# Routed experts of a mixture layer: the up product with stationary weights from two ScalarE-filled buffers, token weights applied at the last eviction

## The chip, the cores and the metric

The kernel runs on one core of a Trainium2 chip. The metric is the device time of one execution in microseconds (us); the kernel before takes 927.88 us, the median of three runs (925.97, 927.88 and 929.93).

## The reference

Two decoder layers on 16 sequences of 128 tokens with 256 features, all in fp32: linear attention, cross attention, and a routed attention-and-FFN block in the first layer, softmax attention, cross attention and a mixture of experts in the second, with a layer norm after each. The change lies in the mixture of experts. Each of the 2048 tokens goes to 4 of 16 routed experts (group-limited top-k of sigmoid scores, normalised, times 2.5); in addition every token goes through two shared experts of the same size. Cut to what matters:

```
combine = (one_hot(topk_idx, E) * tw[..., None]).sum(1)     # token weight per expert
h = einsum('td,edf->etf', x, gate_w)                        # D = 256, F = 256, E = 16
u = einsum('td,edf->etf', x, up_w)
y = einsum('etf,efd->etd', silu(h) * u, down_w)
routed = einsum('etd,te->td', y, combine)
out = routed + shared
```

The token weight is one number per token and expert, so it may stand on silu(h)*u or on y.

## The kernel before, in words

The program is written engine by engine: each engine has its own in-order list of instructions, and semaphores ("steps") tie the lists together. Everything ahead of the mixture's routed part, and the final sums and layer norms behind it, are the same in both kernels.

**The routed part.** Tokens have been scattered by expert into a DRAM table `grid`, so that the work falls into NSLOT = 79 slots of 128 rows, each with one expert. `f_se` holds the expert number of each slot and `f_src` the tile of the table. All experts' weights lie in SBUF in `W[P, expert, 1536]`: for each of the KC = 2 halves k of the 256 input features, 512 columns (256 of gate, 256 of up), and behind them 2 x 256 columns of down. A slot t goes through these steps:

- SyncE (L794 to L799) reads the tile number into a register (`value_load`, L797) and loads the 128 rows into a ring of 8 buffers.
- PE `q_turn_` (L1579) transposes the rows, two transposes of 128x128 (helper line L1059) into PSUM bank t%2; ScalarE `q_turned_` (L1931, L1934) copies them to `f_xT`.
- PE `q_up_` (L1585) reads the expert number with `value_load` (L1586) and multiplies: `f_xT` is the stationary operand (two tiles of 128x128), the expert's weights are the moving operand, 512 columns wide, read from `W` at an address in a register (helper line L1046). The result, tokens on the partitions, gate in columns 0 to 255 and up in columns 256 to 511, lies in bank 2 + t%2.
- ScalarE `q_silu_` (L1926, L1929) takes the silu of the gate half; VectorE `q_mul_` (L2538, L2542) multiplies it by the up half and by the token weight `s_w`, which VectorE `q_w_` (L2531, L2534) picks out of the row that came with the tokens.
- PE `q_back_` (L1597) transposes the product (two more transposes, L1059) into bank 4 + t%2 and ScalarE `q_backed_` (L1937, L1940) copies it to `f_aT`, since the down product contracts over the 256 hidden features.
- PE `q_down_` (L1603), with a `value_load` of its own (L1604), multiplies `f_aT` (stationary) by the down weights, 256 columns wide, into bank 6 + t%2; VectorE `q_y_` (L2546, L2552) copies that to a ring of 4 buffers and GpSimd `q_scatter_` (L999, L1006) adds it to the rows of `ys` in DRAM by an indirect DMA.

**Order.** `rolled(engine, stages, ...)` (L251) writes an engine's list: in iteration i it emits, in the order of the given list, each stage for slot i minus its lag. The middle slots are a hardware loop that is unrolled 8 times. The lists are

```
PE    (q_up_, 1), (q_back_, 2), (q_turn_, 0), (q_down_, 3)
ACT   (q_silu_, 1), (q_backed_, 2), (q_turned_, 0)
DVE   (q_mul_, 1), (q_w_, 0), (q_y_, 3)
```

so in iteration i PE does up(i-1), back(i-2), turn(i), down(i-3), and ScalarE silu(i-1), backed(i-2), turned(i). A `wait(engine, step, t, 1, back=2)` asks for the step of slot t-2, as a double buffer needs. A first semaphore of a stage is waited for by the instruction itself; an engine does nothing that stands behind a waiting instruction in its list. A fp32 product of one 128x128 stationary tile is issued as two passes, each a weight load (PEld) and a matmul; a transpose is one pass.

Of the kernel before, what the change touches and what calls it, by code (L numbers as in the profile page):

```python
# [22 lines left out]
P = 128  # L23
B = 16
D = 256
KC = D // P
# [19 lines left out]
E = 16  # L46
EF = 256
# [4 lines left out]
NSLOT = B * 4 + E - 1  # L52
# [5 lines left out]
SR, YR, UR = 8, 4, 8  # L58
# [143 lines left out]
def wait(eng, step, t, k, back=0):  # L202

    if t.peeled and t.b + step.turns * step.round < back:
        return
    eng.wait_ge(step.sem, step.at(t, k, back))
# [44 lines left out]
def rolled(eng, stages, start, total):  # L251


    deepest = max(lag for _, lag in stages)

    def iteration(i):
        for stage, lag in stages:
            if 0 <= i - lag < total:
                stage(Slot(i - lag, i - lag, 0))

    for i in range(start):
        iteration(i)
    with eng.Fori(start // UR, total // UR) as j:
        for u in range(UR):
            for stage, lag in stages:
                stage(Slot(UR * j + (u - lag), u - lag, j))
    for i in range(total // UR * UR, total + deepest):
        iteration(i)
# [14 lines left out]
def build(nc, a):  # L283
    out = a["out"]
    with ExitStack() as ctx:
# [6 lines left out]
        def step(name, n, turns=B, tiles=0):  # L292
            return Step(sem(name), n, 0, turns, tiles)

        bank = [ctx.enter_context(nc.psum_tensor(f"bank{i}", [P, 512], F32)) for i in range(8)]
# [4 lines left out]
        rows = sb("rows", [P, N_ROWS])  # L300
# [45 lines left out]
        A = Carve(0)  # L346
# [47 lines left out]
        A = Carve(0)  # L394
# [28 lines left out]
        A = Carve(kx_at)  # L423
        c_oTs = [A(NQ, S) for _ in range(TILES)]
        A = Carve(folded_at)
# [3 lines left out]
        A = Carve(weights_end)  # L429
        c_S = [A(H, S) for _ in range(TILES)]  # L430
        A = Carve(weights_end)
        c_gT = A(FC, TILES * S)
        A = Carve(weights_end)
# [4 lines left out]
        A = Carve(0)  # L438
# [12 lines left out]
        f_xT = A(B, KC, P)  # L451
# [55 lines left out]
        assert A.at <= scores_at + 2 * H * P  # L507
        A = Carve(scores_at)
        f_h = [A(EF) for _ in range(2)]
        f_a = [A(KC * EF)]  # L510
        f_aT = [A(KC, P) for _ in range(2)]
        A = Carve(0)
        t_bn, t_mv = A(B, 6), A(B, 2)
        t_std, t_rstd, t_off, t_shift = A(B), A(B), A(B), A(B)
# [149 lines left out]
        q_xp = step("q_xp", 1, NSLOT)  # L664
        q_xc = step("q_xc", 1, NSLOT)
        q_up = step("q_up", 1, NSLOT)
        q_silu = step("q_silu", 1, NSLOT)
        q_w = step("q_w", 1, NSLOT)
        q_mul = step("q_mul", 1, NSLOT)
        q_ap = step("q_ap", 1, NSLOT)  # L670
        q_ac = step("q_ac", 1, NSLOT)
        q_dp = step("q_dp", 1, NSLOT)
        q_yc = step("q_yc", 1, NSLOT)

# [356 lines left out]
        def _(pe):  # L1031
# [10 lines left out]
            def product(o, lhs, rhs):  # L1042

                n = len(lhs)
                for k in range(n):
                    m = pe.matmul(o, lhs[k], rhs[k], start=k == 0, stop=k == n - 1)  # L1046
                return m
# [9 lines left out]
            def transposes(o, src, n, width):  # L1057
                for k in range(n):
                    m = pe.transpose(o[:, k * width:(k + 1) * width], src(k), ident[0:width, 0:width])  # L1059
                return m  # L1060
# [522 lines left out]
                    .then_inc(q_xp.sem, 1)  # L1583

            def q_up_(t):  # L1585
                e = pe.value_load(f_se[0:1, bass.ds(t.b, 1)], min_val=0, max_val=E - 1)  # L1586
                wait(pe, q_xc, t, 1)
                wait(pe, q_mul, t, 1, back=2)
                if t.peeled and t.b == 0:
                    pe.wait_ge(l_w[0], 16 * 9)  # L1590
                    pe.wait_ge(l_w[1], 16 * 7)
                    wait(pe, h_yc, turn(DONE - 2), 1)
                product(bank[2 + t.p][:], [f_xT[:, t.p, k, :] for k in range(KC)],
                        [W[:, bass.ds(e, 1), 2 * k * EF:2 * (k + 1) * EF].rearrange("p a n -> p (a n)")
                         for k in range(KC)]).then_inc(q_up.sem, 1)

            def q_back_(t):  # L1597
                wait(pe, q_mul, t, 1)
                wait(pe, q_ac, t, 1, back=2)
                transposes(bank[4 + t.p][:, 0:D], lambda k: f_a[0][:, t.p * EF + k * P:t.p * EF + (k + 1) * P], KC, P)\  # L1600
                    .then_inc(q_ap.sem, 1)

            def q_down_(t):  # L1603
                e = pe.value_load(f_se[0:1, bass.ds(t.b, 1)], min_val=0, max_val=E - 1)  # L1604
                wait(pe, q_ac, t, 1)
                wait(pe, q_yc, t, 1, back=2)
                if t.peeled and t.b == 0:
                    wait(pe, h_yc, turn(DONE - 1), 1)
                product(bank[6 + t.p][:, 0:D], [f_aT[t.p][:, k, :] for k in range(KC)],
                        [W[:, bass.ds(e, 1), (4 + k) * EF:(5 + k) * EF].rearrange("p a n -> p (a n)")  # L1610
                         for k in range(KC)]).then_inc(q_dp.sem, 1)

            pe.wait_ge(f_routed, 5)
            rolled(pe, [(q_up_, 1), (q_back_, 2), (q_turn_, 0), (q_down_, 3)], UR, NSLOT)

            def t_down_(b):
                mine = slice((b - DONE) * P, (b - DONE + 1) * P)
# [16 lines left out]
        def _(act):  # L1634
# [299 lines left out]
                act.copy(f_xT[:, t.p], bank[t.p][:, 0:D].rearrange("p (k t) -> p k t", k=KC))\  # L1934
                   .then_inc(q_xc.sem, 1)

            def q_backed_(t):  # L1937
                wait(act, q_ap, t, 1)
                wait(act, q_dp, t, 1, back=2)
                act.copy(f_aT[t.p], bank[4 + t.p][:, 0:D].rearrange("p (k t) -> p k t", k=KC))\  # L1940
                   .then_inc(q_ac.sem, 1)

            wait(act, h_dp, turn(DONE - 1), 1)
            rolled(act, [(q_silu_, 1), (q_backed_, 2), (q_turned_, 0)], UR, NSLOT)

            for u in range(DONE, UNITS):
                h_silu_(turn(u))
# [7 lines left out]
        def _(dve):  # L1955
# [574 lines left out]

            def q_w_(t):  # L2531
                dve.wait_ge(l_sx[t.ring(SR)], 16 * (t.lap(SR) + 1))
                wait(dve, q_mul, t, 1, back=2)
                dve.scalar_tensor_tensor(out=s_pick[t.p], in0=s_x[t.ring(SR)][:, D:D + E], scalar=1.0,  # L2534
                                         in1=f_mine[:, bass.ds(t.b, 1), :].rearrange("p a e -> p (a e)"),
                                         op0=ALU.mult, op1=ALU.mult, accum_out=s_w[t.p]).then_inc(q_w.sem, 1)

            def q_mul_(t):  # L2538
                wait(dve, q_silu, t, 1)
                wait(dve, q_ap, t, 1, back=2)  # L2540
                wait(dve, q_w, t, 1)
                dve.scalar_tensor_tensor(out=f_a[0][:, t.p * EF:(t.p + 1) * EF], in0=f_h[t.p],  # L2542
                                         scalar=s_w[t.p], in1=bank[2 + t.p][:, EF:2 * EF],
                                         op0=ALU.mult, op1=ALU.mult).then_inc(q_mul.sem, 1)

            def q_y_(t):  # L2546
                wait(dve, q_dp, t, 1)
                if not t.peeled or t.b >= YR:
                    dve.wait_ge(l_sy[t.ring(YR)], 16 * t.lap(YR))
                elif t.b >= YR - HR + 2:  # L2550
                    dve.wait_ge(l_hs[t.b - YR + HR], 16 * (DONE // HR))
                dve.tensor_copy(s_y[t.ring(YR)], bank[6 + t.p][:, 0:D]).then_inc(q_yc.sem, 1)  # L2552

            rolled(dve, [(q_mul_, 1), (q_w_, 0), (q_y_, 3)], UR, NSLOT)

            def t_sum_(b):
                dve.wait_ge(l_sx[b // 2], 16 * ((NSLOT + SR - 1 - b // 2) // SR + 1))
# [110 lines left out]
```

## Time and profile before

| what | value |
|---|---|
| median of three runs | 927.88 us (925.97 to 929.93) |
| profiled execution: span, first to last instruction | 927.1 us |
| median minus that span | 0.8 us |
| PE busy over the span | 851.1 us, 92% |
| VectorE, ScalarE, GpSimd busy | 561.4, 438.7, 458.6 us |
| mean granted TensorE clock | 0.980 of 2.4 GHz |
| routed slots: first silu, last silu | 641.09 us, 889.77 us |

The profile has no whole-program time of its own for the profiled execution beside its span; the span is 0.8 us (0.1%) under the median of the runs. In its page, PE is the matmul part of TensorE and PEld its weight loads, which overlap; the end of a matmul is modelled. The timeline merges neighbouring instructions of one line, with the number of them behind an x; in brackets stands how long the engine had been idle and who released it. Views of a line give the number of instructions, the shortest, median and longest duration in ns and the first and the last start.

### The profile page before, as it was taken

Reading aid. Unit: us, or ns where it says so; the run is one execution under the profiler, and the core shown is the slowest. Engines: PE = TensorE matmul, PEld = TensorE weight load, DVE = VectorE, ACT = ScalarE, POOL = GpSimd, SP = SyncE. Lnnn points to the kernel's source line nnn. Section 1 sums busy time; section 2 is a strip of 40 time slices with the busy share of each in tenths; the row PEclk is TensorE's granted clock in tenths of the full one; section 3 lists DMA queues with packets and bytes.
Section 4 is the critical chain, followed back from the end, with each engine's and each line's share of the span. In section 5 each row is a group of like instructions: output and inputs, shape, how many; then the busy total and the mean of one; then the engine's idle time right before and its main releaser. Section 6 shows DMA issues by size and latency. Waiting matters only on the chain.

```text
span 927.1 us, 20122 instructions
## 1 busy us (share of the span) xinstructions
PE 851.1 (92%) x5868; PEld 609.7 (66%) x5869; DVE 561.4 (61%) x1640; ACT 438.7 (47%) x1159; POOL 458.6 (49%) x609
## 2 busy tenths in 40 slices
PE   5989689997988999998999988998899999999995
PEld 2666479875877888887777765555455555555553
DVE  3799638849126989888887898583233333333325
ACT  2556345445526777777777864211232323223224
POOL 3999512103135454633455444777744545454545
PEclk9999989998999999999999999999899999999998
DMA  8610111000039999981511100756445555555547
GB/s 300 197 67 6 34 30 36 24 18 12 24 89 308 290 314 326 277 238 41 201 36 37 36 30 32 273 206 213 103 83 92 84 88 88 85 92 83 94 60 253
DMA packets 86642, 113.50 MB, mean 122 GB/s; under 512 B 8224, under 2 KB 77600, under 8 KB 86048
## 3 DMA queue, kind: packets, MB, share of 16 engines
q1 hardware_dynamic: 71392, 90.49, 32.1%
q0 software_dynamic: 14448, 19.34, 12.9%
q10 hardware_dynamic: 720, 2.63, 0.8%
q8 instruction: 44, 0.72, 0.3%
q14 instruction: 38, 0.31, 0.1%
HBM read 48.40 MB, written 64.05 MB: 121 GB/s over the span
## 4 chain that ended last, share of the span: by engine, by line
PE 71%; DVE 7%; POOL 7%; issue 6%; ACT 4%; DMA 4%; SPq 0%; POOLq 0%; DVEq 0%; ACTq 0%
PE bank L1046 46%; PE bank L1059 7%; PE bank L1522 6%; PE bank L1495 3%; PE bank L1532 3%; POOL arena L896 2%; POOL arena L877 1%; DMA ys<-arena 1%; DMA const<-in_const 1%; DVE arena L2436 1%; POOL arena L872 1%; PE bank L1390 1%; PE bank L1232 1%; PE bank L1038 1%; DMA arena<-ys 1%
## 5 line engine op out<-in xcount | busy, mean ns | idle before, releaser
L1046 PE MATMUL bank<-arena 128*128 (+6 forms) x1344 | 423.1, 455 | 16.8 <-ACT arena L1683 8.9
L1046 PEld LDWEIGHTS bank<-arena 128*128 128x128 f32 (+1 forms) x1344 | 230.3, 191 | 131.1 <-issue 96.2
L1006 POOL DMA_INDIRECT ys<-arena x79 | 123.2, 1559 | 117.3 <-DVE arena L2552 103.0
L2542 DVE SCALAR_TENSOR_TENSOR arena<-arena,bank 128x256 f32<-128x256 f32 x79 | 38.0, 481 | 143.8 <-ACT arena L1929 143.8
L1929 ACT ACTIVATE arena<-bank 128x256 f32<-128x256 f32 x79 | 30.4, 385 | 176.0 <-PE bank L1046 176.0
L1059 PEld LDWEIGHTS bank<-const,arena 128*128 128x128 f32 x572 | 69.7, 142 | 66.3 <-issue 56.8
L855 POOL TENSOR_TENSOR lr<-mv,const 128x1 f32<-128x1 f32 x48 | 9.2, 192 | 187.9 <-DVE mv L1978 187.8
L2436 DVE TENSOR_REDUCE arena<-bank 128x4 f32<-128x512 f32 x128 | 87.0, 680 | 23.7 <-PE bank L1495 12.1
L1059 PE MATMUL bank<-const,arena 128*128 128x128 f32 x572 | 94.2, 277 | 6.6 <-DMA arena<-grid 2.6
L1889 ACT ACTIVATE arena<-arena 128x512 f32<-128x512 f32 x116 | 74.1, 638 | 38.0 <-DVE arena L2442 37.1
L1522 PE MATMUL bank<-const,arena 128*128 128x128 f32 x512 | 79.7, 278 | 4.3 <-ACT arena L1896 3.4
L2442 DVE TENSOR_TENSOR arena<-bank,arena 128x512 f32<-128x512 f32 x116 | 80.3, 692 | 4.0
L1896 ACT COPY arena<-bank 128x512 f32<-128x512 f32 x128 | 75.9, 593 | 12.7 <-PE bank L1522 11.8
L950 POOL DMA_INDIRECT grid<-X,arena x64 | 63.3, 989 | 20.2 <-issue 18.5
L1046 PE MATMUL bank<-arena,inT 128*128 128x256 f32 (+1 forms) x192 | 59.5, 434 | 10.1 <-DMA arena<-in_a_w 5.9
L1522 PEld LDWEIGHTS bank<-const,arena 128*128 128x128 f32 x512 | 56.7, 141 | 18.1 <-issue 13.5
L1046 PE MATMUL bank<-xT,arena 128*128 128x128 f32 x512 | 66.2, 278 | 2.2 <-ACT xT L1655 2.2
L1046 PEld LDWEIGHTS bank<-xT,arena 128*128 128x128 f32 x512 | 61.8, 194 | 3.0 <-ACT xT L1655 3.0
L2552 DVE COPY arena<-bank 128x256 f32<-128x256 f32 x79 | 33.6, 425 | 30.9 <-PE bank L1046 29.0
L1046 PEld LDWEIGHTS bank<-arena,inT 128*128 128x128 f32 x192 | 34.0, 197 | 19.5 <-issue 11.9
L974 POOL TENSOR_TENSOR arena<-arena,const 128x256 f32<-128x256 f32 x64 | 38.1, 616 | 5.0 <-ACT arena L1871 5.0
L1532 PE MATMUL bank<-arena 128*32 128x128 f32 x1024 | 34.6, 275 | 3.4 <-ACT arena L1896 3.2
(288 smaller groups left out, 1339.1 us busy)
## 6 DMA issues: line engine op xcount, KB each, us to landing
grid<-arena SPq DMA_DIRECT2D x1, 37264.0 KB, 132.0
arena<-in_f_w SPq DMA_DIRECT2D x18, 768.0 KB, 7.2
arena<-grid SPq DMA_DIRECT2D x79, 137.0 KB, 2.7
arena<-ys SPq DMA_DIRECT2D x8, 512.0 KB, 8.0
inT<-in_ctxT SPq DMA_DIRECT2D x30, 128.0 KB, 2.0
X<-in_x SPq DMA_DIRECT2D x1, 2048.0 KB, 15.6
arena<-in_c_w SPq DMA_DIRECT2D x2, 1024.0 KB, 5.0
ys<-arena SPq DMA_DIRECT2D x1, 2048.0 KB, 10.3
```

Source lines behind the costliest of these rows:

```text
L950: pool.indirect_dma_start(grid, bass.IndirectOffsetOnAxis(ap=f_to[:, b, k:k + 1], axis=0), X[:, b, :], None).then_inc(l_sc[b % 3], 16)
L974: pool.tensor_tensor(d_kx[t.p][:, k], kT[:, k:k + 1, :].to_broadcast([P, 2, P]), c("pairs").unsqueeze(2).to_broadcast([P, 2, P]), ALU.mult ...
L1006: pool.indirect_dma_start(ys, bass.IndirectOffsetOnAxis(ap=number, axis=0), s_y[t.ring(YR)], None, compute_op=ALU.add).then_inc(l_sy[t.rin ...
L1046: m = pe.matmul(o, lhs[k], rhs[k], start=k == 0, stop=k == n - 1)
L1059: m = pe.transpose(o[:, k * width:(k + 1) * width], src(k), ident[0:width, 0:width])
L1522: m = pe.transpose(bank[7][:, i * P:(i + 1) * P], d_S[t.p][:, QH * r + i, :], ident)
L1532: m = pe.matmul(bank[0][32 * i:32 * i + 32, g * P:(g + 1) * P], d_v[t.p][:, QH * g + i, :], d_pT[t.p][:, QH * g + i, :], start=True, stop= ...
L1889: act.activation(v, v, ACT.Exp).then_inc(d_exp.sem, 1)
L1896: act.copy(d_pT[t.p][:, QH * r:QH * (r + 1), :], bank[7][:].rearrange("p (a b) -> p a b", a=QH)).then_inc(d_pTc.sem, 1)
L2436: dve.tensor_reduce(mx, s_, AX.X, ALU.max).then_inc(dm.sem, 1)
L2442: dve.tensor_tensor(d_S[t.p][:, QH * r:QH * (r + 1), :], s_, mx.unsqueeze(2).to_broadcast([P, QH, P]), ALU.subtract).then_inc(dm.sem, 1)
L2542: dve.scalar_tensor_tensor(out=f_a[0][:, t.p * EF:(t.p + 1) * EF], in0=f_h[t.p], scalar=s_w[t.p], in1=bank[2 + t.p][:, EF:2 * EF], op0=ALU ...
```

## The change

The up product changes operands: 128x128 pieces of the expert's gate and up weights become the stationary operand and the transposed tokens the moving one, so its result has the hidden features on the partitions and feeds the down product without the transposes back. The stationary pieces are read from two fixed buffers `f_up[t%2]` (in the space of `rows`, no longer used by then), into which ScalarE copies the 1024 gate and up columns of the expert, at an address that it reads itself with `value_load`. The token weight moves from the product of silu and up to the eviction of the down product. `q_back_` and `q_backed_` are gone, the down product's lag is 2 in place of 3.

```diff
-        f_a = [A(KC * EF)]
         f_aT = [A(KC, P) for _ in range(2)]
+        f_up = [rows[:, i * 2 * KC * EF:(i + 1) * 2 * KC * EF] for i in range(2)]
...
             def q_up_(t):
-                e = pe.value_load(f_se[0:1, bass.ds(t.b, 1)], min_val=0, max_val=E - 1)
                 wait(pe, q_xc, t, 1)
+                wait(pe, q_wc, t, 1)
                 wait(pe, q_mul, t, 1, back=2)
...
-                product(bank[2 + t.p][:], [f_xT[:, t.p, k, :] for k in range(KC)],
-                        [W[:, bass.ds(e, 1), 2 * k * EF:2 * (k + 1) * EF].rearrange("p a n -> p (a n)")
-                         for k in range(KC)]).then_inc(q_up.sem, 1)
-
-            def q_back_(t):
-                wait(pe, q_mul, t, 1)
-                wait(pe, q_ac, t, 1, back=2)
-                transposes(bank[4 + t.p][:, 0:D], lambda k: f_a[0][:, t.p * EF + k * P:t.p * EF + (k + 1) * P], KC, P)\
-                    .then_inc(q_ap.sem, 1)
+                for half in range(2):
+                    for part in range(KC):
+                        at = half * EF + part * P
+                        m = product(bank[2 + t.p][:, at:at + P],
+                                    [f_up[t.p][:, 2 * k * EF + at:2 * k * EF + at + P] for k in range(KC)],
+                                    [f_xT[:, t.p, k, :] for k in range(KC)])
+                m.then_inc(q_up.sem, 1)

             def q_down_(t):
                 e = pe.value_load(f_se[0:1, bass.ds(t.b, 1)], min_val=0, max_val=E - 1)
-                wait(pe, q_ac, t, 1)
+                wait(pe, q_mul, t, 1)
                 wait(pe, q_yc, t, 1, back=2)
...
-            rolled(pe, [(q_up_, 1), (q_back_, 2), (q_turn_, 0), (q_down_, 3)], UR, NSLOT)
+            rolled(pe, [(q_up_, 1), (q_turn_, 0), (q_down_, 2)], UR, NSLOT)
...
-            def q_backed_(t):
-                wait(act, q_ap, t, 1)
-                wait(act, q_dp, t, 1, back=2)
-                act.copy(f_aT[t.p], bank[4 + t.p][:, 0:D].rearrange("p (k t) -> p k t", k=KC))\
-                   .then_inc(q_ac.sem, 1)
+            def q_weights_(t):
+                if t.peeled and t.b == 0:
+                    act.wait_ge(f_routed, 5)
+                    act.wait_ge(l_w[0], 16 * 9)
+                    act.wait_ge(l_w[1], 16 * 7)
+                e = act.value_load(f_se[0:1, bass.ds(t.b, 1)], min_val=0, max_val=E - 1)
+                wait(act, q_up, t, 1, back=2)
+                act.copy(f_up[t.p], W[:, bass.ds(e, 1), 0:2 * KC * EF].rearrange("p a n -> p (a n)")).then_inc(q_wc.sem, 1)

-            rolled(act, [(q_silu_, 1), (q_backed_, 2), (q_turned_, 0)], UR, NSLOT)
+            rolled(act, [(q_silu_, 1), (q_turned_, 0), (q_weights_, 0)], UR, NSLOT)
...
             def q_w_(t):
                 dve.wait_ge(l_sx[t.ring(SR)], 16 * (t.lap(SR) + 1))
-                wait(dve, q_mul, t, 1, back=2)
+                wait(dve, q_yc, t, 1, back=2)
...
             def q_mul_(t):
                 wait(dve, q_silu, t, 1)
-                wait(dve, q_ap, t, 1, back=2)
-                wait(dve, q_w, t, 1)
-                dve.scalar_tensor_tensor(out=f_a[0][:, t.p * EF:(t.p + 1) * EF], in0=f_h[t.p],
-                                         scalar=s_w[t.p], in1=bank[2 + t.p][:, EF:2 * EF],
-                                         op0=ALU.mult, op1=ALU.mult).then_inc(q_mul.sem, 1)
+                wait(dve, q_dp, t, 1, back=2)
+                dve.tensor_tensor(f_aT[t.p], f_h[t.p].rearrange("p (k t) -> p k t", k=KC),
+                                  bank[2 + t.p][:, EF:2 * EF].rearrange("p (k t) -> p k t", k=KC), ALU.mult)\
+                   .then_inc(q_mul.sem, 1)
...
-                dve.tensor_copy(s_y[t.ring(YR)], bank[6 + t.p][:, 0:D]).then_inc(q_yc.sem, 1)
-
-            rolled(dve, [(q_mul_, 1), (q_w_, 0), (q_y_, 3)], UR, NSLOT)
+                wait(dve, q_w, t, 1)
+                dve.tensor_scalar(s_y[t.ring(YR)], bank[6 + t.p][:, 0:D], s_w[t.p], None, ALU.mult).then_inc(q_yc.sem, 1)
+
+            rolled(dve, [(q_mul_, 1), (q_y_, 2), (q_w_, 0)], UR, NSLOT)
```

## Rows read from the trace of the kernel before

**Rows 1.** The page: busy time by engine, and its shares of 40 slices.

```profile
PE 851.1 (92%) x5868; PEld 609.7 (66%) x5869; DVE 561.4 (61%) x1640; ACT 438.7 (47%) x1159; POOL 458.6 (49%) x609
...
PE   5989689997988999998999988998899999999995
```

**Rows 2.** Windows: span, busy (count) of PE, PEld, DVE, ACT, POOL, clock, DMA.

```profile
700.00:880.00 180.00, 180.00 (x696) 105.81 (x695) 57.93 (x232) 53.62 (x174) 89.89 (x59) 1.00 0.54 87
```

**Rows 3.** Timeline of one slot: start, duration, engine, line, count.

```profile
700.30 0.37 ACT L1940 COPY arena<-bank 128x256 f32<-128x256 f32 x1
...
700.55 0.39 ACT L1934 COPY arena<-bank 128x256 f32<-128x256 f32 x1
...
702.91 0.60 PE L1059 MATMUL bank<-const,arena 128*128 128x128 f32 x4
...
703.11 0.39 ACT L1929 ACTIVATE arena<-bank 128x256 f32<-128x256 f32 x1 [2.17 <-PE bank L1046]
...
703.35 1.03 PE L1046 MATMUL bank<-arena 128*128 x4
703.39 0.37 ACT L1940 COPY arena<-bank 128x256 f32<-128x256 f32 x1
703.53 0.48 DVE L2542 SCALAR_TENSOR_TENSOR arena<-arena,bank 128x256 f32<-128x256 f32 x1 [1.78 <-ACT arena L1929]
```

**Rows 4.** Timeline in an attention stage: eight 128-column fp32 passes in a row.

```profile
455.10 1.06 PE L1046 MATMUL bank<-xT,arena 128*128 128x128 f32 x8
```

**Rows 5.** Groups by line and form: busy us, mean ns, idle before.

```profile
L1059 PE MATMUL bank<-const,arena 128*128 128x128 f32 x572 | 94.2, 277 | 6.6 <-DMA arena<-grid 2.6 <-DVE arena L2046 2.0 <-ACT arena L1903 1.1
L1046 PE MATMUL bank<-arena 128*128 128x256 f32 x336 | 84.8, 387 | 10.4 <-ACT arena L1683 8.9 <-DVE arena L2397 1.5
...
L1046 PE MATMUL bank<-arena 128*128 128x512 f32 x160 | 72.2, 594 | 0.0
L1046 PE MATMUL bank<-xT,arena 128*128 128x128 f32 x512 | 66.2, 278 | 2.2 <-ACT xT L1655 2.2
```

**Rows 6.** Groups of ScalarE: the rows nearest to a copy of 1024 columns.

```profile
L1896 ACT COPY arena<-bank 128x512 f32<-128x512 f32 x128 | 75.9, 593 | 12.7 <-PE bank L1522 11.8
L1889 ACT ACTIVATE arena<-arena 128x512 f32<-128x512 f32 x116 | 74.1, 638 | 38.0 <-DVE arena L2442 37.1
...
L1655 ACT COPY xT<-bank 128x256 f32<-128x256 f32 x48 | 18.2, 379 | 10.6 <-PE bank L1038 5.5 <-PE bank L1059 5.0
```

**Rows 7.** SyncE's value load (L797) and what uses its register (L798).

```profile
L797 SPq TENSOR_LOAD <-arena x79: 262/267/816, 633.1 to 877.8; - x79
L797 SPq FUSED_REGOPS  x79: 152/152/173, 633.6 to 878.1; - x79
L797 SPq SEQ_ASSERT  x79: 18/18/33, 633.8 to 878.3; - x79
...
L798 SPq MOVE arena<-grid x79: 29/29/37, 634.0 to 878.5; - x79
```

**Rows 8.** PE's value loads between 700 and 880 us.

```profile
L1586 PEldq TENSOR_LOAD <-arena x58: 296/301/314, 699.9 to 877.1; - x58
...
L1604 PEldq TENSOR_LOAD <-arena x58: 298/578/711, 701.5 to 878.9; - x58
```

**Rows 9.** Timeline: the first slots, from the first copy to ScalarE's first silu.

```profile
638.54 0.37 ACT L1934 COPY arena<-bank 128x256 f32<-128x256 f32 x1 [8.32 <-PE bank L1059]
...
639.07 1.98 PE L1046 MATMUL bank<-arena 128*128 x4 [0.62 <-ACT arena L1934]
...
641.09 0.39 ACT L1929 ACTIVATE arena<-bank 128x256 f32<-128x256 f32 x1 [2.17 <-PE bank L1046]
```

**Rows 10.** Timeline: the last silu and the last eviction of a down product.

```profile
889.77 0.39 ACT L1929 ACTIVATE arena<-bank 128x256 f32<-128x256 f32 x1 [2.17 <-PE bank L1046]
...
893.79 0.42 DVE L2552 COPY arena<-bank 128x256 f32<-128x256 f32 x1 [0.58 <-PE bank L1046]
```

**Rows 11.** Timeline: the one interruption of the rhythm.

```profile
662.64 0.39 ACT L1929 ACTIVATE arena<-bank 128x256 f32<-128x256 f32 x1 [2.34 <-PE bank L1046]
...
665.35 0.69 PE L1059 MATMUL bank<-const,arena 128*128 128x128 f32 x2 [2.61 <-DMA arena<-grid]
...
671.87 0.39 ACT L1929 ACTIVATE arena<-bank 128x256 f32<-128x256 f32 x1 [5.42 <-PE bank L1046]
```

**Rows 12.** Windows: stretches in which PE has idle time (columns as in rows 2).

```profile
90.00:98.00 8.00, 4.92 (x31) 3.65 (x29) 7.79 (x23) 5.14 (x17) 5.40 (x7) 1.00 0.13 36
...
102.00:112.00 10.00, 7.75 (x38) 5.94 (x37) 6.79 (x21) 3.94 (x10) 4.87 (x8) 1.00 0.00 0
...
286.00:290.00 4.00, 2.54 (x20) 2.00 (x19) 3.90 (x9) 2.16 (x5) 0.45 (x2) 1.00 0.80 270
...
666.00:672.00 6.00, 5.69 (x11) 3.13 (x11) 0.42 (x1) 0.51 (x2) 3.51 (x3) 0.50 0.69 120
```

More of the change, by code:

```diff
@@ L666, in build @@
         q_up = step("q_up", 1, NSLOT)
+        q_wc = step("q_wc", 1, NSLOT)
         q_silu = step("q_silu", 1, NSLOT)
@@ L669, in build @@
         q_mul = step("q_mul", 1, NSLOT)
-        q_ap = step("q_ap", 1, NSLOT)
-        q_ac = step("q_ac", 1, NSLOT)
         q_dp = step("q_dp", 1, NSLOT)
@@ L1585, in q_up_ @@
             def q_up_(t):
-                e = pe.value_load(f_se[0:1, bass.ds(t.b, 1)], min_val=0, max_val=E - 1)
                 wait(pe, q_xc, t, 1)
+                wait(pe, q_wc, t, 1)
                 wait(pe, q_mul, t, 1, back=2)
                 if t.peeled and t.b == 0:
-                    pe.wait_ge(l_w[0], 16 * 9)
-                    pe.wait_ge(l_w[1], 16 * 7)
                     wait(pe, h_yc, turn(DONE - 2), 1)
-                product(bank[2 + t.p][:], [f_xT[:, t.p, k, :] for k in range(KC)],
-                        [W[:, bass.ds(e, 1), 2 * k * EF:2 * (k + 1) * EF].rearrange("p a n -> p (a n)")
-                         for k in range(KC)]).then_inc(q_up.sem, 1)
-            def q_back_(t):
-                wait(pe, q_mul, t, 1)
-                wait(pe, q_ac, t, 1, back=2)
-                transposes(bank[4 + t.p][:, 0:D], lambda k: f_a[0][:, t.p * EF + k * P:t.p * EF + (k + 1) * P], KC, P)\
-                    .then_inc(q_ap.sem, 1)
+                for half in range(2):
[5 more added lines that the diff above has]
+                m.then_inc(q_up.sem, 1)
             def q_down_(t):
                 e = pe.value_load(f_se[0:1, bass.ds(t.b, 1)], min_val=0, max_val=E - 1)
-                wait(pe, q_ac, t, 1)
+                wait(pe, q_mul, t, 1)
                 wait(pe, q_yc, t, 1, back=2)
```

## The prediction

> **What bounds the kernel now.** I read the page first: PE is busy for 92% of the span, and in the last third of the slices, where the routed slots lie, for 90% or more [rows 1]. Then the windows of the routed part: from 700 to 880 us PE is busy for all of 180 us, at the full clock (1.00, the 2.4 GHz level), while ScalarE works 53.6 us, a third [rows 2]. Then the timeline of one slot. PE's dynamic matmuls of slot after slot begin 3.09 us apart, silu after silu too, and ScalarE waits 2.17 us for PE before each silu [rows 3]. So a slot costs what PE needs for it, and every wait of another engine lies under PE. Over the whole part the first silu starts at 641.09 and the last at 889.77 us [rows 9, 10]: 248.7 us for 78 steps, of which one step of 9.23 us (662.64 to 671.87) is an interruption [rows 11]: PE had to wait 2.61 us for a load of rows, and then worked at half clock.
>
> **What PE gains.** The passes of a slot before: up 4 of 512 columns, transposes 4, down 4 of 256. Four transposes take 0.44 us from the first of them to the matmul behind (702.91 to 703.35), so 0.11 us each; four down passes last 1.03 us with the last one's 0.39 us whole, so 0.215 each and about 0.87 together [rows 3, 5]; a 512-column pass costs 72.2/160 = 0.45 us by its group, or 3.09 - 0.44 - 0.87 = 1.78 us for four [rows 3, 5]. After: up is 8 products of 128 columns, 16 passes. The nearest row is eight such fp32 passes with a new weight tile for each: 1.06 us with the last one's 0.28 us whole, so 0.111 us each [rows 4], and 16 cost 1.78 us. Splitting the product is thus free, the doubled weight loads hide behind the matmuls, and what goes is the two transposes back: 0.22 us a slot, 17 us over 79 slots, if PE stayed the bound. Bounds of the pass: 0.11 (a transpose) to 0.13 us (66.2/512 over the whole group, tails included) [rows 5], so 1.76 to 2.1 us for up.
>
> **What takes its place.** ScalarE's list is in order: silu(i-1), turned(i), weights(i). PE's up(i) needs the weights of slot i, and silu(i-1) needs the whole up(i-1). So the copy of the next slot's weights stands behind a silu that waits for the slot in work. The two buffers don't help: the copy would be free to start two slots ahead, but it is queued behind that wait. The loop is up(i-1), then silu or the transposes, then turned(i), then the value load, then the copy, then up(i), once per slot. I add it up from the start of up(i-1):
>
> - up, 16 passes at 0.111: 1.78 us [rows 4].
> - turn(i), two transposes: the second starts 0.11 later and lasts 0.27; the transposed rows are there at 2.16 us [rows 3, 5]. The silu starts at 1.95 + 0.03 and blocks the engine for 0.28 us only (the next ScalarE instruction starts 0.28 us after it [rows 3]), so turned(i) goes at 2.16 + 0.03 (the hop from an end to the waiting engine: 703.11 + 0.39 to 703.53 [rows 3]) = 2.19.
> - The value load stands behind turned(i) in the list and starts when that is let go. On SyncE it is 0.27 + 0.15 + 0.02 us of instructions, and 0.7 us pass from the start of the load (877.8) to the instruction behind (878.5) [rows 7]. I take 0.75 us, with one register operation ahead for the index. Ends: 0 hidden behind turned's own work (see the rivals), 1.05 if the load takes 0.58 us.
> - The copy of 1024 columns: no row has that width. From 256 to 512 columns a copy grows from 0.379 to 0.593 us, 0.84 us per 1000 columns; to 1024 that gives 1.02 us, from the row with its source in SBUF (0.638) 1.07 us [rows 6]. I take 1.04, and 0.07 us for its start. Ends: 1.0, and 1.19 for twice the row of 512.
> - From the end of a ScalarE copy to PE's matmul: 638.54 + 0.37 to 639.07, 0.15 us [rows 9].
>
> Sum: 2.19 + 0.75 + 0.07 + 1.04 + 0.15 = 4.20 us a slot against 3.09. PE's own work, 1.78 + 0.22 + 0.87 = 2.87 us, fits under it with about 1.3 us idle. PE's one remaining value load (down) runs behind the transposes during ScalarE's part: 2.0 + 1.0 (a load of 0.58 and SyncE's 0.43 for what follows it, [rows 7, 8]) + 0.87 = 3.9 us at worst, still under 4.20.
>
> Of the value load, the rows show 0.267 us on SyncE and 0.30 or 0.58 us at the median at PE's two places [rows 7, 8]; my sum uses the first. The Trainium skill (DMA: Bandwidth & Descriptors, Latency and other measured facts) puts a floor of about 600 ns under a tensor_load. The rows are below that floor; by the page the sum would be 0.33 us a slot higher, an estimate of 1033 us.
>
> **The rest of the change.** VectorE: the multiply loses its scalar and keeps 128x256 (0.48 us), the eviction gains one (0.42 us before [rows 10]); both are one pass over the same elements. VectorE has 57.9 of 180 us of work [rows 2], so it stays covered; if that cover went, 0.1 us would stand in each place. The multiply ends at about 1.98 + 0.42 + 0.48 = 2.9, before down(i-1) of the next round. GpSimd's scatter comes once per 4.2 us in place of 3.09 and has more room; SyncE's loads keep their 8 buffers. ScalarE's work per slot becomes 0.39 + 0.39 + 1.04 us, under half of 4.20: it isn't full, it is in the chain. A longer slot also swallows the interruption: slot 8's rows arrived at 665.35 [rows 11], while PE would ask for them only after 640.6 + 8 x 4.20 = 674 us. That step becomes an ordinary one; the sum below counts it so.
>
> At the front the first up waits for the first weights: 638.57 + 0.75 + 0.07 + 1.04 + 0.15 = 640.6 in place of 639.07 [rows 9], +1.5 us. At the end the last eviction starts 4.0 us after the last silu [rows 10]; with one stage less I take 3.0, -1 us (between -2 and 0).
>
> Total: 78 x 4.20 = 327.6, minus 248.7 is +78.9; +1.5 - 1.0 gives +79.4. The span goes from 927.1 to 1006.5; the median lies 0.8 us above the span, so about 1007 us.
>
> **Rivals.**
>
> *The value load is hidden (15%).* ScalarE's sequencer might run it while silu and turned(i) are in work. For it: their durations overlap (0.25 us from copy to copy, each 0.37 or more [rows 3]). Against: the load stands behind an instruction that waits for the transposes. Then the slot is 1.95 + 0.03 + 0.28 + 0.25 + 1.04 + 0.15 = 3.70 us, +40 us: 968.
>
> *The value load is slow on ScalarE (12%).* PE's second one has a median of 0.578 us [rows 8]; 0.28 us more per slot, 78 x 0.28 = +22: 1029.
>
> *The clock falls (7%).* PE would idle some 1.3 us in each slot. In the trace, the clock went to 0.50 (1.2 GHz) after PE had stood for 2.61 us [rows 11, 12]. Stretches with shorter gaps kept 1.00: PE busy 61% at 90 to 98 us, 78% at 102 to 112, 64% at 286 to 290 [rows 12]; the new slot would be near 70%. At half clock passes double: 2.19 becomes about 4.1 and the slot 6.1 us, 1155 if it never recovers, about 1080 if half the time. The Trainium skill (TensorE: Matmul & The Clock Gate, A second HAM failure mode: psum-queue depth-cycling) tells of a kernel whose clock oscillates because PE idles briefly and often between groups of matmuls, which would speak against this change; the three rows at 1.00 don't bear it out.
>
> *PE stays the bound, and the kernel gets faster (3%).* If the copy of slot i ran while PE works on up(i-1), the slot would be 2.87 us and the 0.06 us that 3.09 holds over its 3.03 of passes (with 1.72 for up): 2.93. 78 x 2.93 = 228.5, and the interruption's 6.1 us stay: 14 us less, 913 us. The mechanism is that of the two buffers; it decides once the copy is ready before PE has done turn(i) and down(i-2). Against it stands ScalarE's order, which leaves no way round the silu. The same with a slot near 3.1 us gives no change (1%).
>
> **How the numbers follow.** Forecast 62%, slot 3.9 to 4.5 us: 984 to 1031, likeliest 1007. A tenth of a us in the slot is 7.8 us. The range of 8 in 10 takes in the hidden load and the slow one: 966 to 1036, leaving out the clock, the faster case and the outer parts of the forecast. 0.5% of 927.9 (4.6 us) is about what a measurement of this kernel can tell from no change. Slower 0.96, within it 0.01, faster 0.03.
>
> **What the profile after would show.** Right: silus 4.2 us apart; before each up pass PE idle about 0.5 to 1.3 us, released by ScalarE's copy of 1024 columns; that copy 1.0 to 1.1 us; a value load on ScalarE's queue between turned and the copy; PE busy near 75% from 700 us on with the clock at 1.00; the wait for rows at 662 us gone. The chain of waits should name ScalarE's copy where it named PE alone. Wrong: silus 3.7 us apart or less (load hidden); PE idle before down rather than before up (PE's own value load binds); a clock below 1.00; or a ScalarE that copies weights before silu's wait is over.

## The result, and the profile after

The changed kernel takes 1017.85 us (median of 4 runs, 1015.5 to 1019.05), the kernel before 928.61 us beside it; the ratio is 1.0957, 95% interval 1.0936 to 1.0978. The forecast was 1007 us in a range of 966 to 1036.

The page of the changed kernel, busy time by engine and PE's shares of 40 slices, against [rows 1]:

```profile
PE 852.2 (84%) x6658; PEld 680.5 (67%) x6659; DVE 567.4 (56%) x1640; ACT 498.6 (49%) x1160; POOL 457.8 (45%) x609
...
PE   6998699979989999999998999777777777777786
```

PE works as long as before, 852 against 851 us, in a span that is 90 us longer: its share in the routed part has gone from 9 and over to 7 tenths. The two transposes that are gone don't show in that sum: a burst of passes that ends in idle time counts its last pass whole, and there is one such burst per slot now. The windows of that part, against [rows 2] (span, then busy time and count of PE, PEld, DVE, ACT, POOL, then the clock and DMA):

```profile
700.00:960.00 260.00, 186.56 (x1322) 160.97 (x1321) 65.27 (x240) 101.52 (x180) 93.35 (x61) 1.00 0.39 63
```

PE is busy 72% of the time, ScalarE 39%: no engine is full, which is what a chain across engines looks like. The clock stayed at 1.00 in these 260 us. It didn't at the front of the part: PE had stood idle for 2.20 us before 642.74 and for 1.87 us after 644.98, and from 647.8 to 651.2 us the clock was at the 1.2 GHz level:

```profile
648.00:652.00 4.00, 3.61 (x15) 2.96 (x13) 0.77 (x2) 1.69 (x3) 3.09 (x4) 0.60 0.53 177
```

The first two steps from silu to silu took 4.97 and 4.51 us, the three behind them 4.07 or 4.08. The timeline of one slot, one with the median load, against [rows 3]:

```profile
760.09 2.02 PE L1045 MATMUL bank<-arena,rows 128*128 128x128 f32 x16 [1.18 <-issue]
...
761.95 0.38 PE L1058 MATMUL bank<-const,arena 128*128 128x128 f32 x2
...
762.15 0.38 ACT L1924 ACTIVATE arena<-bank 128x256 f32<-128x256 f32 x1 [2.16 <-PE bank L1045]
762.17 1.03 PE L1045 MATMUL bank<-arena 128*128 x4
762.43 0.37 ACT L1929 COPY arena<-bank 128x256 f32<-128x256 f32 x1
...
763.25 1.04 ACT L1939 COPY rows<-arena 128x1024 f32 x1 [0.45 <-issue]
...
764.39 2.02 PE L1045 MATMUL bank<-arena,rows 128*128 128x128 f32 x16 [1.19 <-issue]
```

PE finishes down's passes at 763.20 (762.17 + 1.03) and then has nothing for 1.19 us, until ScalarE's copy of the 1024 weight columns (L1939), 763.25 to 764.29, is done. ScalarE had waited 2.16 us for the up product before the silu (L1924), then copied the transposed rows (L1929), and stood 0.45 us in "issue" before the copy of the weights: that is the value load and its register work, as far as they reach beyond the copy of the rows. The chain of waits of one slot shows the same sequence (start, duration, what):

```profile
705.42 0.04 ACT arena L1924
...
705.70 0.00 issue
705.70 0.37 ACT arena L1929
706.07 0.22 ACTq L1937
...
706.32 0.15 ACTq L1937
...
706.50 0.02 ACTq L1937
...
706.56 0.06 ACTq L1939
...
706.66 1.05 ACT rows L1939
707.71 0.23 issue
707.94 2.05 PE bank L1045 x16
```

"ACTq" is ScalarE's sequencer: the tail of the value load (L1937), its register work, the address of the copy (L1939). From 706.07 to 706.66 the engine has nothing to do and waits for it. Then the copy, then PE. ScalarE's value load and copy in all 79 slots (count: shortest/median/longest ns):

```profile
L1937 ACTq TENSOR_LOAD <-arena x79: 275/420/629, 640.7 to 978.5; - x79
...
L1939 ACT COPY rows<-arena x79: 1044/1044/1046, 641.6 to 979.4; 128x1024 f32 x79
```

First and last silu, against [rows 9, 10], and the front of the part:

```profile
640.63 0.37 ACT L1929 COPY arena<-bank 128x256 f32<-128x256 f32 x1 [8.32 <-PE bank L1058]
...
642.74 2.02 PE L1045 MATMUL bank<-arena,rows 128*128 128x128 f32 x16 [2.20 <-issue]
...
644.79 0.38 ACT L1924 ACTIVATE arena<-bank 128x256 f32<-128x256 f32 x1 [2.16 <-PE bank L1045]
...
982.63 0.38 ACT L1924 ACTIVATE arena<-bank 128x256 f32<-128x256 f32 x1 [2.16 <-PE bank L1045]
...
984.79 0.48 DVE L2550 TENSOR_SCALAR arena<-bank,arena 128x256 f32<-128x256 f32 x1 [0.81 <-PE bank L1045]
```

From silu to silu: 337.84 us over 78 steps, 4.33 us each, against 248.68 before: +89.2. The first copy of rows came at 640.63 in place of 638.54, so this execution was 2.1 us late before anything that was changed. From that copy to the first silu it takes 4.16 us in place of 2.55, +1.6; from the last silu to the last eviction 2.16 in place of 4.02, -1.9. Sum 89.2 + 2.1 + 1.6 - 1.9 = 91.0 up to the last eviction; the spans differ by 90.1.

### The profile page after: what moved, and what is told of

The parts are those of the page before. It is cut to its first block, busy times and chain, and to the rows that moved or that the text cites. A ratio compares the mean times of both kernels' runs of the same rounds, so it can differ in the third digit from the quotient of the medians.

```text
span 1017.2 us, 21543 instructions
## 1 busy us (share of the span) xinstructions
PE 852.2 (84%) x6658; PEld 680.5 (67%) x6659; DVE 567.4 (56%) x1640; ACT 498.6 (49%) x1160; POOL 457.8 (45%) x609
## 4 chain that ended last, share of the span: by engine, by line
PE 69%; issue 13%; DVE 7%; ACT 5%; POOL 4%; DMA 1%; ACTq 0%; POOLq 0%; SPq 0%; DVEq 0%
PE bank L1045 47%; PE bank L1521 5%; PE bank L1058 5%; PE bank L1494 3%; PE bank L1531 3%; POOL arena L895 1%; DMA const<-in_const 1%; DVE arena L2434 1%; ACT rows L1939 1%; POOL arena L876 1%; PE bank L1389 1%; PE bank L1231 1%; PE bank L1037 1%; POOL arena L871 1%; ACT arena L1829 1%
## 5 line engine op out<-in xcount | busy, mean ns | idle before, releaser
L1045 PE MATMUL bank<-arena 128*128 128x256 f32 (+6 forms) x1028 | 279.1, 406 | 12.9 <-ACT arena L1678 7.4
L1045 PE MATMUL bank<-arena,rows 128*128 128x128 f32 x1264 | 160.9, 280 | 96.7 <-issue 83.9
L1045 PEld LDWEIGHTS bank<-arena,rows 128*128 128x128 f32 x1264 | 147.9, 192 | 126.0 <-issue 126.0
L1045 PEld LDWEIGHTS bank<-arena 128*128 128x128 f32 (+1 forms) x1028 | 177.4, 192 | 70.4 <-issue 35.7
L2539 DVE TENSOR_TENSOR arena<-arena,bank 128x256 f32<-128x256 f32 x79 | 33.3, 422 | 219.5 <-ACT arena L1924 219.5
L1924 ACT ACTIVATE arena<-bank 128x256 f32<-128x256 f32 x79 | 30.4, 384 | 173.5 <-PE bank L1045 173.5
L1939 ACT COPY rows<-arena 128x1024 f32 x79 | 82.5, 1045 | 35.0 <-issue 35.0
L1521 PE MATMUL bank<-const,arena 128*128 128x128 f32 x512 | 80.6, 280 | 4.2 <-ACT arena L1891 3.2
L1058 PE MATMUL bank<-const,arena 128*128 128x128 f32 x414 | 76.1, 279 | 4.0 <-DVE arena L2044 2.0
L1521 PEld LDWEIGHTS bank<-const,arena 128*128 128x128 f32 x512 | 57.3, 142 | 17.9 <-issue 13.4
L1058 PEld LDWEIGHTS bank<-const,arena 128*128 128x128 f32 x414 | 50.0, 142 | 20.7 <-issue 14.7
L2550 DVE TENSOR_SCALAR arena<-bank,arena 128x256 f32<-128x256 f32 x79 | 38.2, 483 | 23.5 <-PE bank L1045 23.5
```

The source lines that it names most:

```text
L1521: m = pe.transpose(bank[7][:, i * P:(i + 1) * P], d_S[t.p][:, QH * r + i, :], ident)
L1939: act.copy(f_up[t.p], W[:, bass.ds(e, 1), 0:2 * KC * EF].rearrange("p a n -> p (a n)")).then_inc(q_wc.sem, 1)
L2539: dve.tensor_tensor(f_aT[t.p], f_h[t.p].rearrange("p (k t) -> p k t", k=KC), bank[2 + t.p][:, EF:2 * EF].rearrange("p (k t) -> p k t", k=K ...
L2550: dve.tensor_scalar(s_y[t.ring(YR)], bank[6 + t.p][:, 0:D], s_w[t.p], None, ALU.mult).then_inc(q_yc.sem, 1)
```

## Experiments

**Copy first.** The one edit puts ScalarE's copy ahead of the silu that waits for the product in work.

```diff
-            rolled(act, [(q_silu_, 1), (q_turned_, 0), (q_weights_, 0)], UR, NSLOT)
+            rolled(act, [(q_weights_, 0), (q_silu_, 1), (q_turned_, 0)], UR, NSLOT)
```

> The changed kernel with one edit: ScalarE's list begins with the copy of the next slot's weights, then the silu, then the transposed rows. Theory (the copy is slow only because it stands behind a silu that waits for the whole up product): value load and copy (1.8 us) run while PE works on up(i-1), PE is the bound again at 2.95 us a slot (16 passes at 0.111, two transposes, four down passes, 0.06 left over). The interruption at slot 8 comes back, since the rows arrive when they arrive, so silu 8 stays near 672 us and 70 slots follow: 672 + 70 x 2.95 = 878, 11 us earlier than before, and 2 us less at the end: about 915 us, a little under the kernel before. Rival (stationary weights themselves are dear, by weight loads or by memory traffic of the copy): the slot stays at 3.5 us or above, 950 us or more.

Measured: 906.65 us (905.67 to 907.56), ratio to before 0.9769 (0.9735 to 0.9803): 111 us faster than the changed kernel, and about 21 us, 2.0 to 2.7%, faster than the kernel before. The timeline of a slot and the windows:

```profile
751.65 0.39 ACT L1924 ACTIVATE arena<-bank 128x256 f32<-128x256 f32 x1 [0.87 <-PE bank L1045]
751.67 1.03 PE L1045 MATMUL bank<-arena 128*128 x4
751.94 0.37 ACT L1929 COPY arena<-bank 128x256 f32<-128x256 f32 x1
...
752.54 1.95 PE L1045 MATMUL bank<-arena,rows 128*128 128x128 f32 x16
752.61 1.04 ACT L1939 COPY rows<-arena 128x1024 f32 x1 [0.30 <-issue]
...
754.52 0.39 ACT L1924 ACTIVATE arena<-bank 128x256 f32<-128x256 f32 x1 [0.87 <-PE bank L1045]
```

```profile
700.00:860.00 160.00, 160.00 (x1228) 153.11 (x1227) 61.03 (x224) 94.85 (x168) 86.71 (x56) 1.00 0.57 95
```

The copy (752.61 to 753.65) now runs under the up passes (752.54 to 754.49); PE is busy 160.00 of 160 us; silus are 2.87 us apart. That is the sum 1.78 + 0.22 + 0.87 of the prediction with nothing left over. The 16 up passes take 1.95 us here and 2.02 where PE comes out of idle time. Stationary weights, the doubled weight loads and the traffic of the copy cost PE nothing: the rival of this run has fallen. The run came out 8 us under its expectation, since the slot was 2.87 and not 2.95 (-6), and the interruption was shorter:

```profile
664.53 0.43 PE L1058 MATMUL bank<-const,arena 128*128 128x128 f32 x2 [1.81 <-DMA arena<-grid]
```

PE waited 1.81 us where it had waited 2.61 [rows 11], the step was 5.63 us in place of 9.23, and the clock held:

```profile
664.00:668.00 4.00, 2.92 (x20) 2.58 (x21) 0.67 (x3) 1.42 (x2) 2.53 (x2) 1.00 0.73 129
668.00:676.00 8.00, 8.00 (x63) 7.68 (x63) 3.09 (x11) 4.87 (x9) 5.30 (x4) 1.00 0.77 119
```

**Copy first, half the copy.**

```diff
-                act.copy(f_up[t.p], W[:, bass.ds(e, 1), 0:2 * KC * EF]...)
+                act.copy(f_up[t.p][:, 0:KC * EF], W[:, bass.ds(e, 1), 0:KC * EF]...)
```

> The order with the copy first (906.65 us), but only 512 of the 1024 columns copied (the weights for the second half of the input features are left out). Theory: PE is the bound and the copy lies under it, so the 0.43 us less change nothing: 906.6 within 2 us, slot 2.87. Rival (the copy still takes part in the bound, through ScalarE or through memory traffic that slows PE): 5 us or more faster.

Measured: 910.42 us (908.76 to 911.16), ratio 0.9803 (0.9781 to 0.9824). Less work and 3.8 us slower than the run that it was made from, so outside both expectations. The slot is the same, 2.868 us at the median and as the mean of all steps from the 15th on, in both; the copy is indeed hidden. The two profiled executions differ by 4.4 us, and that comes from elsewhere: the first silu starts at 644.15 in place of 642.15 us, and from silu to silu it is 229.44 in place of 227.10 us, because of the interruption:

```profile
667.32 0.43 PE L1058 MATMUL bank<-const,arena 128*128 128x128 f32 x2 [3.21 <-DMA arena<-grid]
```

```profile
664.00:668.00 4.00, 0.55 (x4) 0.20 (x2) 2.13 (x8) 0.59 (x2) 2.84 (x2) 1.00 0.73 100
668.00:676.00 8.00, 7.69 (x46) 7.21 (x47) 1.78 (x7) 2.37 (x7) 5.15 (x5) 0.79 0.69 120
```

PE stood for 3.21 us in place of 1.81 and the clock fell to the 1.2 GHz level for part of the 8 us behind; the step took 8.58 us. The rows of slot 8 are loaded only after GpSimd has scattered the result of slot 0 (`load_slot`), and that stands in GpSimd's list behind its scatters of the tokens, outside the change: the last of these starts at 655.74 us in the run with the whole copy and at 658.84 in this one. All four runs of this kernel are slower than all four of the other, but only one of each has a profile, and why wasn't tried. The two kernels ran in different sets of runs; the kernel before took 928.15 us beside the first and 928.49 beside the second, so the sets themselves don't differ by that much.

**Load first.** ScalarE's value load alone goes ahead of the silu; the copy keeps its place.

```diff
-            rolled(act, [(q_silu_, 1), (q_turned_, 0), (q_weights_, 0)], UR, NSLOT)
+            rolled(act, [(q_load_, 0), (q_silu_, 1), (q_turned_, 0), (q_weights_, 0)], UR, NSLOT)
```

The new `q_load_` holds the `value_load` that stood in `q_weights_`.

> The changed kernel with ScalarE's value load alone taken ahead of the silu; silu, transposed rows and copy keep their order. Theory (value load and copy both stand in the chain of a slot): the load, measured at 0.28 to 0.63 us with 0.35 us of register work behind it, goes under PE's up product, and the slot falls from 4.33 by 0.65 to 0.8 us to about 3.6: 1017.9 - 78 x 0.7 = 963 us. Rival (the load is hidden by ScalarE's own work already and the copy alone is the price): within 5 us of 1018.

Measured: 975.53 us (973.73 to 975.75), ratio 1.0502 (1.0464 to 1.054).

```profile
750.54 0.39 ACT L1924 ACTIVATE arena<-bank 128x256 f32<-128x256 f32 x1 [2.16 <-PE bank L1045]
...
750.82 0.37 ACT L1929 COPY arena<-bank 128x256 f32<-128x256 f32 x1
...
751.07 1.06 ACT L1945 COPY rows<-arena 128x1024 f32 x1
...
752.23 2.02 PE L1045 MATMUL bank<-arena,rows 128*128 128x128 f32 x16 [0.64 <-issue]
```

The copy of weights now starts 0.25 us after that of the rows, where it took 0.82 us (762.43 to 763.25) before, and the slot is 3.75 us. So 42 of the 90 us were the value load and its registers: the load was in the chain, its rival has fallen. The 47 us that are left over the kernel before are the loop with the copy in it. The expectation was 963 us, 12 us less than measured: the 0.25 us that one ScalarE instruction takes to follow the other stay when the load goes. This slot is close to the 3.70 us that the prediction gave for a hidden load.

**Half the copy, in the order of the change.**

```diff
-                act.copy(f_up[t.p], W[:, bass.ds(e, 1), 0:2 * KC * EF]...)
+                act.copy(f_up[t.p][:, 0:KC * EF], W[:, bass.ds(e, 1), 0:KC * EF]...)
```

> The changed kernel, but only the first 512 of the 1024 columns are copied for a slot (the part of the weights for the second half of the input features is left out, so the products are not the reference's). Theory: half the copy, 512 columns at 0.84 us per 1000, is 0.43 us less in the chain of each slot: 1017.9 - 78 x 0.43 = 984 us. Rival (the end of the copy is not what PE waits for, the memory traffic or the value load of PE is): within 5 us of 1018.

Measured: 974.21 us (972.12 to 975.32), ratio 1.0497 (1.046 to 1.0535).

```profile
L1939 ACT COPY rows<-arena x79: 617/617/619, 639.9 to 933.2; 128x512 f32 x79
```

The copy is 0.43 us shorter (1.044 to 0.617), as said, but the slot 0.57 us (4.33 to 3.76), so the run came out 10 us under its 984. The rest is the value load: its median went from 0.42 to 0.28 us without any edit to it. That raised the question of the next run but one.

**The token weight alone.** The kernel before, with the weight at the eviction. Since the weight is now used two slots later, `s_w` and `s_pick` also get four buffers in place of two, and `q_w_` waits for the eviction four slots back in place of the multiply two back (not in the diff below).

```diff
-                dve.scalar_tensor_tensor(out=f_a[0][...], in0=f_h[t.p], scalar=s_w[t.p], in1=bank[2 + t.p][:, EF:2 * EF],
-                                         op0=ALU.mult, op1=ALU.mult).then_inc(q_mul.sem, 1)
+                dve.tensor_tensor(f_a[0][...], f_h[t.p], bank[2 + t.p][:, EF:2 * EF], ALU.mult).then_inc(q_mul.sem, 1)
...
-                dve.tensor_copy(s_y[t.ring(YR)], bank[6 + t.p][:, 0:D]).then_inc(q_yc.sem, 1)
+                wait(dve, q_w, t, 1)
+                dve.tensor_scalar(s_y[t.ring(YR)], bank[6 + t.p][:, 0:D], s_w[t.r % 4], None, ALU.mult).then_inc(q_yc.sem, 1)
```

> The kernel before with one part of the change alone: the token weight is applied at the eviction of the down product, and the multiply of silu and up loses it. Theory: both lie under PE, which stays busy all the time, so 928 us, within 2 us. Rival (the eviction grows by 0.06 us and frees the scatter later, or VectorE's order delays the multiply): 3 us or more slower.

Measured: 928.57 us (926.34 to 930.33), ratio 0.9998 (0.9979 to 1.0017). Under a busy PE this part of the change costs and gives nothing.

**No scatter.**

```diff
-                pool.indirect_dma_start(ys, ..., s_y[t.ring(YR)], None, compute_op=ALU.add).then_inc(l_sy[t.ring(YR)], 16)
+                pool.sem_inc(l_sy[t.ring(YR)], 16)
```

> The changed kernel without GpSimd's indirect DMAs of the routed part (the adding of the routed outputs to the result is left out; their semaphores are set by a plain increment). Theory, from the trace of the changed kernel: ScalarE's value load takes long (up to 0.63 us) when it starts 2.0 to 2.5 us after the start of a scatter, and ends then at about 2.65 us after it, so the scatter holds it up. Without scatters every load takes 0.27 to 0.29 us, the median falls from 0.42, and the slot from 4.33 to 4.15: 1017.9 - 78 x 0.17 = 1004 us. Rival (the load is slow because of the passes of PE or of the multiply that run at the same time): median load still near 0.42 us and 1015 to 1020 us.

Measured: 1006.68 us (1005.66 to 1007.96), ratio 1.0838 (1.0816 to 1.0859), 11 us under the changed kernel; the slot is 4.19 us.

```profile
L1935 ACTq TENSOR_LOAD <-arena x79: 273/280/484, 640.4 to 967.4; - x79
```

PE, VectorE and ScalarE do the same work at the same places, and the load is 0.28 us at the median in place of 0.42. So GpSimd's scatter holds up ScalarE's value load, and that is 11 us of the result. Whether it does so by its instruction or by its transfers, which went with it, this run can't tell.

**Copy in the middle.** Ahead of the transposed rows, still behind the silu.

```diff
-            rolled(act, [(q_silu_, 1), (q_turned_, 0), (q_weights_, 0)], UR, NSLOT)
+            rolled(act, [(q_silu_, 1), (q_weights_, 0), (q_turned_, 0)], UR, NSLOT)
```

> The changed kernel with ScalarE's list as silu, copy of the weights, transposed rows. Theory (what costs is to stand behind the silu): load and copy start 0.2 us earlier, but the transposed rows now stand behind the copy and PE waits for them: 1.95 + 0.03 + 0.75 + 0.07 + about 0.95 to the start of the next instruction + 0.37 + 0.15 = 4.3 us a slot, 1010 to 1025 us. Rival (standing behind the wait for the transposes is what costs): the copy is out of the chain and the slot falls below 3.9 us, under 985.

Measured: 1021.16 us (1019.99 to 1024.08), ratio 1.1003 (1.0974 to 1.1032), the slot 4.37 us.

```profile
802.24 0.39 ACT L1924 ACTIVATE arena<-bank 128x256 f32<-128x256 f32 x1 [2.14 <-PE bank L1045]
803.25 1.04 ACT L1939 COPY rows<-arena 128x1024 f32 x1 [0.64 <-issue]
804.21 0.37 ACT L1929 COPY arena<-bank 128x256 f32<-128x256 f32 x1
```

The order behind the silu hardly matters (0.04 us a slot): PE then waits for the rows, L1929, which end last. What costs is to stand behind the silu.

**One buffer.**

```diff
-        f_up = [rows[:, i * 2 * KC * EF:(i + 1) * 2 * KC * EF] for i in range(2)]
+        f_up = [rows[:, 0:2 * KC * EF] for i in range(2)]
...
-                wait(act, q_up, t, 1, back=2)
+                wait(act, q_up, t, 1, back=1)
```

> The changed kernel with both slots' weights in one buffer, the copy waiting for the product of the slot before in place of the one two slots back. Theory (the copy stands behind a silu that needs the same product anyway): the second buffer is never used to run ahead, so nothing changes, within 3 us of 1018. Rival (the second buffer does cover something): 5 us or more slower.

Measured: 1016.62 us (1015.74 to 1018.13), ratio 1.0952 (1.0929 to 1.0975), the same as with two within the expected 3 us. In the order of the change the second buffer buys nothing, since the silu ahead of the copy already waits for the product that frees the first one.

## Why the prediction was right

- **The bound before and PE's gain.** Right. The gain was there to be had, as the run with the copy first shows: a slot of 2.87 us, the predicted sum, against 3.09, and 21 us less in all. Of these, 3.6 us are the shorter interruption, which the edit didn't aim at.
- **The chain.** Right. The loop up, silu, transposed rows, value load, copy, up was shown by moving single members of it: the copy ahead of the silu (-111 us), the load ahead (-42), half the copy (-44), and by two edits that should and did change nothing much (copy in the middle +3, one buffer -1).
- **Its size.** The sum said 4.20 us a slot, the trace has 4.33; over 78 steps that is 10 of the 11 us from 1007 to 1018. The mis-sized term is the first one, from up's start to the copy of the rows: 2.19 in the sum, 2.35 measured (mean of slots 15 to 74; 760.09 to 762.43 in the slot above). Not quite half of it is a slip in the sum. It let that copy wait for the transposes alone, at 2.19, while the silu ahead of it, at 1.98 and blocking the engine for 0.28, lets it go only at 2.26; the rival of a hidden load uses that path. The rest is the first pass of up: out of idle time it is 0.185 us from its start to that of the second one and not 0.111, and the silu starts at 2.07. The other terms, as means of the same slots: from the start of the rows' copy to that of the weights' copy 0.82 for 0.75 + 0.07; the weights' copy 1.04 for 1.04; from its end to PE 0.12 for 0.15. Together 2.35 + 0.82 + 1.04 + 0.12 = 4.33.
- **The value load** was right in that sum by luck. The load itself took 0.42 us at the median where SyncE's 0.27 had been taken [rows 7], and from its end to the copy it was 0.37 us, where the sum had left 0.55 (0.75 + 0.07 - 0.27); the two errors cancel. So the rival of a slow load was half true. Its cost is real, 11 us by the run without scatters, but it isn't what the prediction missed.
- **Front, end, interruption.** +1.6 for +1.5 us, -1.9 for -1.0, and the wait for rows at slot 8 is gone, as expected. The 2.1 us by which this execution was late ahead of the routed part belong to no term; among the runs of the experiments the first silu lies between 642.15 and 644.42 us with the same code ahead of the routed part.
- **The token weight.** Costed at nothing, and nothing it was (ratio 0.9998).
- **The rival of the clock.** The clock stayed at 1.00 from 651.2 us to the end of the routed part, with PE idle for about 1.2 us in each slot, so the time bears the forecast out. The rival was argued from three rows at 1.00, though, and the same trace has rows with gaps under 2.61 us where it fell: after PE had stood for 1.77 us at 96.79, and for 2.03 us at 222.92:

```profile
98.00:102.00 4.00, 3.44 (x12) 3.07 (x13) 1.53 (x6) 1.61 (x5) 1.71 (x5) 0.58 0.00 0
...
222.00:230.00 8.00, 5.14 (x32) 3.24 (x31) 7.79 (x13) 4.25 (x9) 5.40 (x6) 0.68 0.00 0
```

  Gaps of about 1.8 us came out both ways (1.77 here, 1.81 with the copy first, where the clock held), so the 7% had less behind it than it seemed, and the changed kernel did run 3.4 us at the lower level at its front, as did the run with the copy first (0.57 from 640 to 644 us). A repeated oscillation, as the Trainium skill tells of it for one kernel (TensorE: Matmul & The Clock Gate, A second HAM failure mode: psum-queue depth-cycling), shows in the routed part of no run here.
- **The other rivals.** The Trainium skill's floor of about 600 ns for a tensor_load (DMA: Bandwidth & Descriptors, Latency and other measured facts) is reached only by the slowest loads: 275 to 629 ns on ScalarE. The rival in which PE stays the bound needed another order of ScalarE's list; with that order it came out at 906.65 us, where the prediction had 913.

## What to carry to other kernels

Where an engine's list is in order, a prefetch is only as early as its place in the list: ask which wait stands ahead of it, and whether that wait needs the work that the prefetch should run under. A second buffer is of use only if it lets the copy pass that wait, and a quick test for it is to take the second buffer away (that was done here in the order of the change alone, not with the copy first). A value load counts in a chain with its register work, 0.65 to 1.0 us from its start to the copy here, and putting it alone ahead of the wait took 42 us off.

## What was not expected of the hardware

The value load's time depends on when it falls after GpSimd's indirect scatter. Two slots of the changed kernel, the scatter's start and the load (L1937, one each):

```profile
799.35 1.56 POOL L1005 DMA_INDIRECT ys<-arena  x1 [2.95 <-DMA ys<-arena]
```

```profile
L1937 ACTq TENSOR_LOAD <-arena x1: 511/511/511, 801.5 to 801.5; - x1
```

```profile
794.85 1.56 POOL L1005 DMA_INDIRECT ys<-arena  x1 [2.51 <-DMA ys<-arena]
```

```profile
L1937 ACTq TENSOR_LOAD <-arena x1: 287/287/287, 797.3 to 797.3; - x1
```

The first starts 2.1 us after its scatter and takes 0.51, the second 2.5 us after and takes 0.29. Of the 46 loads that start 2.0 to 2.4 us after a scatter's start, 43 end between 2.62 and 2.77 us after it, whenever they began. The four that start 1.27 to 1.76 us after one take 0.28, and so do five of the six from 2.49 us on. The kernel before shows the same pattern: PE's load for the down product took 0.58 us at the median, the one for the up product 0.30 [rows 8]; the first starts 2.07 us after a scatter at the median, the second within 0.9 us of one in 54 of 57 cases. For ScalarE's load the run without scatters shows that the scatter is the cause; for PE's it is argued from the pattern. By what path a scatter holds a load up was not tried. It also makes such a term unsteady: a slot's length moves the load in or out of the stretch, as the half copy did (there 65 of 73 loads start less than 1.9 us after a scatter), which won 0.14 us beside its own 0.43.
